# Causal attention layer of a six-layer decoder: where the turn of head 1 stands, and which engine evacuates the turned rows

## The reference

```
def _L1_attn_ref(x, Wq, Wk, Wv, Wo):
    Q = (x @ Wq.T).reshape(b, s, 16, 16).transpose(0, 2, 1, 3)
    K = (x @ Wk.T).reshape(b, s, 4, 16).transpose(0, 2, 1, 3)
    V = (x @ Wv.T).reshape(b, s, 4, 16).transpose(0, 2, 1, 3)
    K = jnp.repeat(K, 4, axis=1); V = jnp.repeat(V, 4, axis=1)
    scores = jnp.einsum('bhqd,bhkd->bhqk', Q, K) / jnp.sqrt(jnp.float32(16))
    scores = jnp.where(causal, -jnp.inf, scores)
    weights = jax.nn.softmax(scores, axis=-1)
    ctx = jnp.einsum('bhqk,bhkd->bhqd', weights, V)
    return ctx.transpose(0, 2, 1, 3).reshape(b, s, 256) @ Wo.T

x = _layernorm(x + _L1_attn_ref(x, ...), axis=-1)   # the fourth sublayer
# the fifth starts with a second layer norm of its input, with weights ln_w, ln_b
```

## Time and profile before

| what | value |
|---|---|
| median of 3 runs | 1497.68 us (1497.03, 1497.68, 1503.88) |
| profiled execution, its own time | 1503.7 us |
| its span, first to last instruction | 1502.0 us |
| busy over the span: PE, DVE, ACT, POOL | 90%, 72%, 62%, 57% |
| mean granted TensorE clock | 0.957 of full speed |
| the causal layer | about 233 to 398.4 us of the span |

### The profile page before, as it was taken

The page is one execution under the profiler, slowest core; times in us unless marked ns, Lnnn a source line. Parts: engine busy times, 40 slices in busy tenths (PEclk is TensorE's granted clock), DMA queues, the critical chain, the costliest instruction groups (busy, mean ns, idle before and its releaser), DMA issues. The chain is left out here.

```text
span 1502.0 us, 27995 instructions
## 1 busy us (share of the span) xinstructions
PE 1358.5 (90%) x8279; PEld 1100.2 (73%) x8296; DVE 1076.8 (72%) x2562; ACT 928.6 (62%) x3126; POOL 856.0 (57%) x988
## 2 busy tenths in 40 slices
PE   8599468889679999999999999999999987999992
PEld 3444356666348999999988888888888865888881
DVE  1599676889668888888898788887888857333332
ACT  3189315777548878788887777777776646222222
POOL 2377103777316767677797676766756632455443
PEclk9699779999789999999999999999999999999997
DMA  3363111000010101001001010010000147233324
GB/s 127 105 245 126 41 27 43 2 1 1 2 43 1 43 2 40 15 2 47 12 23 54 2 43 1 7 37 1 2 1 20 37 165 249 43 50 54 53 43 126
DMA packets 46324, 72.75 MB, mean 48 GB/s; under 512 B 4285, under 2 KB 32901, under 8 KB 43877
## 3 DMA queue, kind: packets, MB, share of 16 engines
q1 hardware_dynamic: 33316, 44.00, 8.8%
q0 software_dynamic: 7488, 10.23, 4.2%
q10 hardware_dynamic: 5376, 16.78, 2.9%
HBM read 50.94 MB, written 20.05 MB: 47 GB/s over the span
## 5 line engine op out<-in xcount | busy, mean ns | idle before, releaser
L1550 ACT ACTIVATE pr_<-ps,neg_ 128x128 f32<-128x128 f32 x512 | 180.9, 365 | 74.3 <-DVE neg_ L1667 73.4
L1608 POOL TENSOR_TENSOR rstd<-var,half 128x6 f32<-128x6 f32 x128 | 172.3, 1346 | 10.0
L1567 ACT ACTIVATE y<-ps,invsm 128x128 bf16<-128x128 f32 x512 | 145.5, 368 | 25.7 <-PE ps L1481 25.5
L1603 POOL TENSOR_TENSOR var<-stat,deps 128x6 f32<-128x6 f32 x128 | 25.4, 198 | 226.3 <-DVE stat L1647 226.3
L1619 POOL TENSOR_TENSOR z<-t,m 128x512 fp32r<-128x512 f32 x128 | 148.6, 1161 | 1.7 <-DVE t L1693 1.7
L1463 PE MATMUL ps<-qkt 128*128 128x128 f32 x1024 | 145.4, 285 | 2.3 <-ACT qkt L1534 1.2
L1463 PEld LDWEIGHTS ps<-qkt 128*128 128x128 f32 x1024 | 124.8, 192 | 29.6 <-issue 26.9
L1492 PE MATMUL ps<-phi,z 128*128 128x256 f32 x512 | 137.9, 301 | 0.7 <-POOL z L1619 0.5
L1612 POOL TENSOR_TENSOR pr_<-pr_,rec_ 128x512 f32<-128x512 f32 x128 | 133.2, 1040 | 3.4 <-DVE rec_ L1674 3.4
L1481 PE MATMUL ps<-XT 128*128 128x256 f32 x512 | 132.1, 380 | 0.7 <-ACT XT L1558 0.6
L1492 PE MATMUL ps<-plo,z 128*128 128x256 f32 x512 | 127.6, 282 | 0.0
(11 more groups left out here) (326 smaller groups left out, 3928.7 us busy)
## 6 DMA issues: line engine op xcount, KB each, us to landing
centred<-raw_weights ACTq DMA_DIRECT2D x8, 1024.0 KB, 4.0
w_low<-w_dram SPq DMA_DIRECT2D x8, 1024.0 KB, 9.6
aw_st<-centred SPq DMA_DIRECT2D x7, 1024.0 KB, 5.0
raw_weights<-wself_dram ACTq DMA_DIRECT2D x4, 1024.0 KB, 10.4
raw_weights<-wcross_dram ACTq DMA_DIRECT2D x4, 1024.0 KB, 15.4
w<-w_dram SPq DMA_DIRECT2D x2, 2048.0 KB, 19.6
aw_rows<-wproj_dram SPq DMA_DIRECT2D x7, 512.0 KB, 3.9
xin<-xT_dram SPq DMA_DIRECT2D x4, 512.0 KB, 8.5
```

The lines of the kernel that those rows point to most:

```text
L1550: ins = act.activation(pr[:, u.par, h, :], bS[:, h * S:(h + 1) * S], ACT.Exp, bias=neg[:, u.par, h:h + 1], accum_out=tot[:, u.par, h:h + 1])
L1567: ins = act.activation(y[:, u.par, h * S:(h + 1) * S], bO[:, h * S:(h + 1) * S], ACT.Copy, scale=invsm[:, head:head + 1])
L1608: pool.tensor_tensor(rstd[:, u.par, 0:6], v, half[:, :], ALU.pow).then_inc(s_rstd, 1)
```

## The change

PE turns heads 1, 2 and 3 of a sequence together, directly behind the next step's scores; head 1 so leaves the place between the masks of heads 2 and 3 for one that is one step later. In DVE's queue the copy of head 1 moves ahead of head 2's, and head 3's moves behind the reciprocal of head 0. `turned_row` leaves DVE: ACT does it, as `activation(Identity)` with scale and bias, one step after its transpose, ahead of `rows_scaled` and the exponentials. Since two engines now evacuate the two banks, PE's wait for a free bank asks for the semaphore of the one that emptied it (`bank_left`).

```
-        turns = [(h, step - lag) for step in range(B + 6) for h, lag in ((2, 3), (3, 3), (ROW, 6), (0, 2), (1, 2))
+        turns = [(h, step - lag) for step in range(B + 6) for h, lag in ((1, 3), (2, 3), (3, 3), (ROW, 6), (0, 2))
+        copies = list(itertools.accumulate(h != ROW for h, _ in turns))
+        def bank_left(eng, n):
+            if n >= 2 and turns[n - 2][0] == ROW:
+                eng.wait_ge(s_rowed, turns[n - 2][1] + 1)
+            elif n >= 2:
+                eng.wait_ge(s_cp, copies[n - 2])
@@ PE: turn, turn_row, context
-                            if n >= 2:
-                                pe.wait_ge(s_cp, n - 1)
+                            bank_left(pe, n)
...
-                    pe.wait_ge(s_cp, n - 1)
+                    bank_left(pe, n)
...
-                    pe.wait_ge(s_cp, turn_no[HKV - 1, u.b] + 1)
+                    pe.wait_ge(s_cp, copies[turn_no[HKV - 1, u.b]])
-                batches([(scores, 2), (turn((2, 3)), 3), (project, 0), (turn_row, 6), (context, 3), (turn((0,)), 2), (masks((0, 1)), 1), (out, 3),
-                         (masks((2,)), 1), (turn((1,)), 2), (masks((3,)), 1)])
+                batches([(scores, 2), (turn((1, 2, 3)), 3), (project, 0), (turn_row, 6), (context, 3), (turn((0,)), 2), (masks((0, 1)), 1),
+                         (out, 3), (masks((2, 3)), 1)])
@@ ACT
-                batches([(values, 1), (rows_scaled, 5), (high, 1), (exps, 2)])
+                def turned_row(u):
+                    n = turn_no[ROW, u.b]
+                    act.wait_ge(s_tp, n + 1)
+                    for k in range(CB):
+                        ins = act.activation(XT[:, k, u.b * S:(u.b + 1) * S], bT[n % 2][:, k * P:(k + 1) * P], ACT.Identity,
+                                             bias=col("lnb", k), scale=col("lnw", k))
+                    ins.then_inc(s_rowed, 1)
+                batches([(values, 1), (turned_row, 7), (rows_scaled, 5), (high, 1), (exps, 2)])
@@ DVE
-                def turned_row(u):
...
-                batches([(row_moments, 4), (row_normed, 5), (maximum(0), 2), (turned(2), 3), (maximum(1), 2), (turned(3), 3), (maximum(2), 2), (reciprocal(0), 2),
-                         (maximum(3), 2), (keys, 0), (queries, 0), (turned_row, 6), (reciprocal(1), 2), (context, 3), (turned(0), 2), (reciprocal(2), 2),
-                         (residual, 3), (statistics, 3), (turned(1), 2), (reciprocal(3), 2)])
+                batches([(row_moments, 4), (row_normed, 5), (maximum(0), 2), (turned(1), 3), (maximum(1), 2), (turned(2), 3), (maximum(2), 2), (reciprocal(0), 2),
+                         (turned(3), 3), (maximum(3), 2), (keys, 0), (queries, 0), (reciprocal(1), 2), (context, 3), (turned(0), 2),
+                         (reciprocal(2), 2), (residual, 3), (statistics, 3), (reciprocal(3), 2)])
```

More of the change, by code:

```diff
@@ L7 @@
+import itertools
 import numpy as np
@@ L790, in causal_layer @@
         lnx = sbuf(ctx, "d_lnx", [P, 2, C], F32)
-        s_row, s_mean, s_power, s_step, s_first, s_second, s_normed, s_lnx = (sem("d_" + n) for n in (
-            "row", "mean", "power", "step", "first", "second", "normed", "lnx"))
+        s_row, s_mean, s_power, s_step, s_first, s_second, s_normed, s_lnx, s_rowed = (sem("d_" + n) for n in (
+            "row", "mean", "power", "step", "first", "second", "normed", "lnx", "rowed"))
         bP, bS, bT, bF = ps[0], ps[1:5], ps[5:7], ps[7]
         ROW = HKV
-        turns = [(h, step - lag) for step in range(B + 6) for h, lag in ((2, 3), (3, 3), (ROW, 6), (0, 2), (1, 2))
+        turns = [(h, step - lag) for step in range(B + 6) for h, lag in ((1, 3), (2, 3), (3, 3), (ROW, 6), (0, 2))
                  if 0 <= step - lag < B]
         turn_no = {turn: i for i, turn in enumerate(turns)}
+        copies = list(itertools.accumulate(h != ROW for h, _ in turns))
[4 more added lines that the diff above has]
+                eng.wait_ge(s_cp, copies[n - 2])
         KEYS, VALUES = C, C + P
@@ L976, in rows_scaled @@
                     act.activation(lnx[:, u.par, :], X[:, u.b, :], ACT.Copy, scale=second[:, u.b:u.b + 1]).then_inc(s_lnx, 1)
-                batches([(values, 1), (rows_scaled, 5), (high, 1), (exps, 2)])
+                def turned_row(u):
[6 more added lines that the diff above has]
+                batches([(values, 1), (turned_row, 7), (rows_scaled, 5), (high, 1), (exps, 2)])
+                act.wait_ge(s_rowed, B)
             @block.vector
@@ L1057, in statistics @@
                     dve.bn_stats(row_stats[:, u.b, :], X[:, u.b, :]).then_inc(s_row, 1)
-                batches([(row_moments, 4), (row_normed, 5), (maximum(0), 2), (turned(2), 3), (maximum(1), 2), (turned(3), 3), (maximum(2), 2), (reciprocal(0), 2),
-                         (maximum(3), 2), (keys, 0), (queries, 0), (turned_row, 6), (reciprocal(1), 2), (context, 3), (turned(0), 2), (reciprocal(2), 2),
-                         (residual, 3), (statistics, 3), (turned(1), 2), (reciprocal(3), 2)])
-                dve.wait_ge(s_cp, len(turns))
+                batches([(row_moments, 4), (row_normed, 5), (maximum(0), 2), (turned(1), 3), (maximum(1), 2), (turned(2), 3), (maximum(2), 2), (reciprocal(0), 2),
+                         (turned(3), 3), (maximum(3), 2), (keys, 0), (queries, 0), (reciprocal(1), 2), (context, 3), (turned(0), 2),
+                         (reciprocal(2), 2), (residual, 3), (statistics, 3), (reciprocal(3), 2)])
+                dve.wait_ge(s_cp, copies[-1])
 def centre_weights(ctx, act, d_raw, d_centred, s_sum, s_mean, s_shift, s_fold, io, sbuf, col, cols):
```

## The result

| | median | lowest to highest | runs |
|---|---|---|---|
| before | 1500.45 us | 1497.03 to 1503.88 | 20 |
| changed | 1503.41 us | 1502.06 to 1509.23 | 20 |

The ratio is 1.0021, 95% interval [1.0013, 1.0028]: 2 to 4 us slower, where 4.6 us less were forecast, and 1503.4 lies outside the range of 1489.5 to 1500. A repetition with 6 runs gave 1.0028 [1.0014, 1.0042]. The forecast of 1493.1 was counted from 1497.7, the median of three runs; with 20 runs the kernel before has its median 2.8 us higher. So of the 10.3 us between forecast and result 2.8 are the starting point, and 7.5 the change: 4.6 not gained and 3 lost.

What follows compares the result with a forecast made beforehand. Loops through several engines were taken to bound the layer's steps: 6 x 0.59 with splitting plus 5 x 0.22 without gave 4.6 us, so 1497.7 - 4.6 = 1493.1 us. Its own range was 1491 to 1495.5, the whole range 1489.5 to 1500.

Steps and rivals of the forecast that it cites:

- The loop of before and the link taken out of it: Steps with splitting: a 9.44 us loop through POOL, PE and DVE; removing DVE's copy of head 1 takes off 0.59.
- POOL loop: Loop through POOL, PE and DVE that sets steps with splitting: 9.44 us before, 8.85 forecast after.
- The bank wait: PE's turn of head 3 waits for DVE's copy of head 1, starting 2.55 us after the scores instead of 2.12.
- The failed step: DVE's first maximum taken to start 1.21 us after the scores, as before, opening the 8.41 us sum.
- bank loop: From scores through DVE's copy of head 1 and PE's queue to the next scores: 8.41 us, setting steps without splitting.
- rival D: The change does not do what it says: bank wait binds every step, 8.85 missed, or a table load appears; chance 0.01.
- Rival B: Gain lost on the way or hidden by the spread, 1496 to 1500 us; chance 0.09.
- Rival C: Slower, 1498 to 1503 us: half clock lasts longer in the layer's start, each 8 us costing up to 4; chance 0.06.
- ACT hides the turned rows: On ACT the pair of turned rows takes 0.63 us within its waits of 2.68 and 2.04 a step, costing nothing.
- Start and drain at nothing: The layer's start (steps 0 to 4) and drain forecast to cost 0 us, with ends of -1.2 and +1.7.

Runs made afterwards that it cites:

- e1: Changed kernel with two neighbouring DVE stages swapped, row_normed ahead of row_moments; 1498.12 us, ratio 0.9991 to the kernel before.
- f3: Changed kernel with POOL's normalise(3) issued as two instructions of 256 columns instead of one of 512; 1499.02 us, ratio 0.9988 to the kernel before.
- f1: The kernel before measured again, unchanged, for a second profile; 1500.98 us, ratio 1.0004.
- e2: Kernel before with only ACT's part: turned rows evacuated by ACT one step later, turns and copies unmoved; 1506.48 us, ratio 1.0054.
- g1: Changed kernel with PE's gaps in step 2 filled by twelve matrix products that nobody reads; 1505.26 us, ratio 1.0027 to the kernel before.
- e3: Kernel before with only the three turns and DVE's copies moved, turned rows still on DVE; 1505.86 us, ratio 1.0043.
- f4: Kernel before with turns moved, turned rows still on DVE, and row_normed ahead of row_moments; 1495.73 us, ratio 0.9974.
- e4: Changed kernel with row_normed half a step earlier, behind the reciprocal of head 2; 1496.38 us, ratio 0.9975 to the kernel before.
- g2: Changed kernel with row_normed half a step earlier, plus PE's gaps in step 2 filled with unread products; 1494.84 us, ratio 0.9953 to the kernel before.

## Why the prediction was wrong

- *The loop of before and the link taken out of it:* right. The POOL loop, freed of both the copy and the hold, is 8.79 (e1) against 8.85 forecast: in e1 POOL pays 0.08 to DVE, and 0.14 was in the row that the forecast was counted from.
- *The bank wait:* right as a mechanism, and it became the bound. Its length without the hold is 8.48 against 8.41; most of the difference is PE's restart, 0.15 from the end of the copy (316.75 + 0.67 to 317.57) where I took 0.05.
- *The failed step* is the first term of the bank loop: "Now: first maximum at 1.21". I took this from the earlier trace rows, where `row_normed` ran 0.1 ahead of POOL, and moved the copy of head 1 without asking what its absence does to the moments and `row_normed` behind it. The first maximum came at 1.83. The term of 0.62, put into the bank loop, gives 9.03, measured 9.08; so six steps gained 0.36 (the first of them 0.52) instead of 0.59, five lost 0.45 instead of gaining 0.22, and the last one went from 8.30 to 8.92. That is -2.3 + 2.2 + 0.6 = +0.5, not -4.6. The earlier trace rows held the sign: POOL's row at 315.82 is 1.18 where its neighbours are 1.04. Something held it, and I passed over it.
- *The rivals.* What the steps did is rival D, which I had put at 0.01: the bank wait binds in every step and 8.85 is not reached. Rival B had the threshold right (the bank loop "must pass 8.85"), and argued against it with steps in which `row_normed` was not held. The outcome lies nearest to C by its sign, but not by C's mechanism in the main.
- The Trainium skill has the rule: "SBUF — State Buffer", section "SBUF: two separate sides", calls the port pair that DVE and POOL share an exclusive lock: when DVE's operation runs in a 2-port performance mode, the one that starts first has the pair for the whole instruction, and the other is blocked. By that rule DVE should wait up to one POOL instruction, 1.04; the trace agrees (0.83 longer), and f3 and e1 show both halves of it. That it is the mode of `row_normed` that makes it subject to the hold was not tested here. I did not draw on that page.
- *ACT hides the turned rows:* right. The pair takes 0.90 (0.63 forecast, between 0.52 and 0.78, so it lies outside), ACT still waits 1.61 for the rows, and no table load came.
- *Rival C*, the longer half clock in the start: right in part, as 0.4 to 1.1 us of the loss (10.19 and 10.10 against 9.71 and 9.07). With the three turns together and no filler it lasted 6.8 us in every one of seven profiles; with the old order of turns 6.8 in the first and 3.4 in f1 and e2. Its price was too high: between the two profiles of before, 3.4 us more of it made the interval 0.64 longer, where C's price was up to 1.7. At equal length (6.8) the changed order still has 0.4 to 0.5 more. In the timeline before, the turn of head 1 fills part of PE's wait for the last exponentials; in the changed kernel that wait is idle (1.01) and the turn comes behind the scores, still at half clock.
- *Start and drain at nothing:* the start costs those 0.4 to 1.1. From the last scores to the end of the layer it takes 27.3 and 25.5 before, 26.8 and 26.6 changed: no difference beyond the spread.
- *What stays open:* the four profiles of the two kernels account for 1.5 us in the layer (168.1 against 166.6), of 2 to 4 measured. Outside of it nothing is changed, and the profiles even point the other way there: between 430 and 450 the clock is at half for about 10 us in the two of before and 3 us in the two of the changed kernel, whose rest is 2.2 us shorter. This does not go with the order of the layer: g1, the changed kernel with filler, has 10 us there too, and e3 and f4 none. So where the other 1 to 2 us come from is not known.

## What to carry to other kernels

Where DVE and POOL both work out of SBUF, look at who starts first: a POOL row or a DVE row longer than its neighbours of the same shape can be a hold, and an order that wins by 0.1 us can be turned over by moving anything in front of it. Before moving an instruction out of an engine's queue, ask what it kept apart, not only what it delayed. Put a DVE operation that can be held clearly ahead of POOL's start (0.16 us in e1 and e4); that swap was worth 5 us here (1503.4 to 1498.1), as much as the change was to bring.

## What the hardware showed that was not expected

- The hold of `row_normed` is for one instruction of the other engine: 1.21 us beside one of 1.04 us, 0.79 beside two of half the size, 0.38 where nothing holds it. The price is lopsided: when DVE is first, POOL pays 0.08 to 0.16; when POOL is first, DVE pays 0.83, or 0.40 behind an instruction of half the size.
- The recorded start alone does not tell the winner: DVE was recorded 0.02 to 0.03 ahead and lost, 0.10 to 0.16 ahead and won. Nothing in between was seen.
- Filling an idle stretch of PE kept its clock at 1.00 there, and falls to 0.50 showed up late in the layer in g1 and g2 (two between 370.9 and 384.5, one from 375.2 to 378.6). That the fill moved them there is not shown. In a kernel with several such gaps a clean stretch is not yet a shorter time.
